# The feed-forward half of a gated cross-attention layer, in four groups of two batches instead of groups of 2, 3 and 3

## The reference, cut to what matters

```python
x = x + tanh(g_xattn) * xattn(ctx, ctx, layernorm(x), Wk, Wv, bv, Wq, bq, Wo, bo)
x = x + tanh(g_ffn) * ffn(layernorm(x), w1, conv_w, conv_b, w2)
# xattn: x is (8, 100, 512), ctx is (8, 722, 512); softmax(q k^T / sqrt(512)) v, one head
def ffn(x, w1, conv_w, conv_b, w2):
    h = bit_linear(x, w1)            # rows quantised to int8 by their largest value, weights to -1, 0, 1
    h = depthwise_conv1d(h)          # 3 taps along the 100 positions of a batch, 2048 channels
    return bit_linear(silu(h), w2)   # the same quantisation, by the largest value of each row of 2048
```

## The kernel before, in words

| section | before | after |
|---|---|---|
| batch 2 | ln2(0), xi, one xqt, rbc(0) | the same (wi(1,3) now stands ahead of the section) |
| batch 3 | second xqt behind res(2); all ff(0), with pt, two kt, pv and three scores between; am1(0) | second xqt and ff(0) from the section's first step, with y, six kt, norm, res(2) and pt between; am1(0) after the first pv; am2(0) after the last; 9 quant(0) among the scores |
| batch 4 | am2(0), 16 quant(0) | 7 quant(0); ln2(1) to rbc(1) at its end |
| batch 5 | ln2(1) to second xqt (three batches) at its end | ff(1) from the first step, with y, kt, norm, res(4), pt, three pv, and f2/out of batches 0 and 1; am1(1), am2(1), 8 quant(1) |
| batch 6 | rbc(1), then behind res(5) all ff(1), with f2/out of batches 0 and 1 and with pt, kt, pv, three scores; am1(1) | 8 quant(1); ln2(2) to first xqt at its end |
| batch 7 | y(6), res(6), am2(1), 16 quant(1) between pt and pv, y(7), res(7) | rbc(2), y(6), res(6), all ff(2) with f2/out of batches 2 and 3, am1(2), pt, two pv, am2(2), 16 quant(2) around the last two pv, y(7), res(7) |
| behind | ln2(2), f2 of batch 2, ff(2) with f2 of batches 3 and 4, am, quant, f2 all of three | ln2(3), f2 of batch 4, ff(3) with f2 of batch 5, am, quant, f2 all of two |

## Time and profile before

### The profile page before, as it was taken

One profiled execution on the slowest core, in us unless ns is written; L12 is line 12 of the kernel. 1 busy time (PEld: TensorE's weight loads), 2 busy tenths in 40 slices (PEclk: granted clock), 3 DMA queues, 4 the chain that ended last, 5 costly groups with the idle time before them and its releaser, 6 DMA issues. The chain is left out here.

```text
span 364.1 us, 4322 instructions
## 1 busy us (share of the span) xinstructions
PE 284.5 (78%) x1496; PEld 202.1 (56%) x1496; DVE 201.2 (55%) x426; ACT 156.3 (43%) x291; POOL 107.0 (29%) x132
## 2 busy tenths in 40 slices
PE   4944999989979989668799996778958575963284
PEld 2414899756537776538578784445826443531142
DVE  0085232330125137669677445679767854798592
ACT  3003137684367552488441324297631102967000
POOL 1007100024210981133226103053321902534090
PEclk9985599999998999957989997898989875887579
DMA  6999129906695259500421600000000000000002
GB/s 191 222 220 330 77 65 294 199 1 154 167 405 132 68 125 229 136 0 3 117 48 21 143 2 0 1 2 23 2 23 0 0 0 24 1 23 3 20 2 68
DMA packets 27952, 32.20 MB, mean 88 GB/s; under 512 B 17866, under 2 KB 17866, under 8 KB 26779
## 3 DMA queue, kind: packets, MB, share of 16 engines
q1 hardware_dynamic: 27930, 31.93, 32.9%
HBM read 26.09 MB, written 1.64 MB: 76 GB/s over the span
## 5 line engine op out<-in xcount | busy, mean ns | idle before, releaser
L861 POOL TENSOR_TENSOR z<-a,ab 128x300 f32<-128x300 f32 (+1 forms) x48 | 33.5, 698 | 77.3 <-DVE a L1076 77.3
L589 PE MATMUL pvb<-pt,ctx 120*128 120x100 f32 (+1 forms) x384 | 45.3, 275 | 1.8 <-ACT pt L743 1.8
L638 PE MATMUL ff<-xqt,w1t 128*128 128x300 bf16 (+1 forms) x192 | 35.4, 333 | 14.1 <-DVE u L1069 12.0
L589 PEld LDWEIGHTS pvb<-pt,ctx 120*128 120x128 f32 (+1 forms) x384 | 44.2, 191 | 3.8 <-issue 3.6
L568 PE MATMUL sc<-kt,qm 128*100 128x361 f32 x128 | 42.4, 480 | 0.0
L804 ACT ACTIVATE a<-u,convb,conv 128x300 f32<-128x300 f32 (+1 forms) x48 | 28.8, 600 | 18.6 <-DVE u L1069 18.6
L872 POOL TENSOR_SCALAR zq<-z_i 128x300 bf16<-128x300 int8 (+1 forms) x48 | 25.6, 558 | 34.9 <-DVE z_i L1114 34.9
L638 PEld LDWEIGHTS ff<-xqt,w1t 128*128 128x128 bf16 x192 | 19.9, 114 | 26.8 <-DVE u L1069 18.8
L549 PE MATMUL tr<-ident,ctx 120*128 120x120 f32 (+1 forms) x192 | 30.0, 281 | 3.9 <-ACT kt L722 3.2
L1076 DVE SCALAR_TENSOR_TENSOR a<-u,conv,a 128x297 f32<-128x297 f32 (+1 forms) x48 | 27.3, 569 | 7.9 <-ACT a L804 7.6
L549 PEld LDWEIGHTS tr<-ident,ctx 120*128 120x128 f32 (+1 forms) x192 | 24.7, 151 | 12.4 <-ACT kt L722 4.2
(11 more groups left out here) (156 smaller groups left out, 474.2 us busy)
## 6 DMA issues: line engine op xcount, KB each, us to landing
ctx<-in_ctx_dram SPq DMA_DIRECT2D x16, 720.0 KB
wraw<-in_L_ffn_w_dram SPq DMA_DIRECT2D x8, 1024.0 KB, 13.4
x_sb<-in_x_dram SPq DMA_DIRECT2D x2, 800.0 KB
out_dram<-x_sb SPq DMA_DIRECT2D x8, 200.0 KB
wq_sb<-in_L_xattn_Wq_dram SPq DMA_DIRECT2D x4, 256.0 KB, 4.3
wk_sb<-in_L_xattn_Wk_dram SPq DMA_DIRECT2D x4, 256.0 KB, 6.4
wv_sb<-in_L_xattn_Wv_dram SPq DMA_DIRECT2D x1, 1024.0 KB, 4.8
wo_sb<-in_L_xattn_Wo_dram SPq DMA_DIRECT2D x1, 1024.0 KB, 7.4
```

Of the source, the lines that this page charges most:

```text
L589: mm = nc.tensor.matmul(pvb[:, k * S:(k + 1) * S], cx[b % NCTX][0:r, i, k * P:(k + 1) * P], pt[0:r, i, :], start=(i == 0), stop=(i == 5))
L638: mm = nc.tensor.matmul(ffb[j % 2][:, 0:w], w1t[:, j * DK + k, :], xqt[:, k, 0:w], start=(k == 0), stop=(k == DK - 1))
L861: nc.gpsimd.tensor_tensor(z[:, j - 1, 0:w].rearrange("p (b s) -> p b s", b=nb), a1[:, n % NBUF, 0:w].rearrange("p (b s) -> p b s", b=nb), ...
```

## The change

The groups become four of two batches. The widest group is then 200 columns instead of 300, and every buffer with that width (`z`, `u`, `a1`, `ab`, `acc_q`, `acc`, `row_wide`, `xqt`, `zq`, `z_i8`, `diag`) shrinks. `z` and the buffers behind it lie over `wraw`, where the w2 weights wait to be turned; `row_wide` now falls into the part that is still being read, so the wait for `w2t_ok` moves from the first `ff` step of group 0 to the first `rbc`. The cuts of `weave` are new.

```diff
-GROUPS = [(0, 2), (2, 5), (5, 8)]
+GROUPS = [(0, 2), (2, 4), (4, 6), (6, 8)]
...
-FILL_CUTS = [17, 22, 33, 50, 71, 88, 100, 116]
+FILL_CUTS = [17, 22, 36, 58, 80, 104, 128, 160]
...
                 elif kind in ("rbc", "am2"):
                     g = step[1]
                     dve.wait_ge(bc_ps, n_bc)
+                    if kind == "rbc" and g == 0:
+
+                        dve.wait_ge(w2t_ok, 16 * CHUNK)
                     nc.vector.tensor_copy(row_wide[:, 0:cols(g)], yb[:, 0:cols(g)]).then_inc(bcast_ok, 1)
...
                     if g == 0 and j == 0:
-
-                        dve.wait_ge(w2t_ok, 16 * CHUNK)
                         nc.vector.memset(ab[:, :, :, S:S + 1], 0.0)
```

## The result

The changed kernel takes 397.59 us (median of four, 397.06 to 402.36) against 366.57 in the same comparison: a ratio of 1.086, with a 95% interval of 1.080 to 1.093. The forecast had the sign, but 380 us and a range to 388. The change costs 31 us, not 14. Some executions of every kernel fall into a slower state (over 1.5% above its fastest); medians are taken over all executions, ratios over the others alone.

A forecast was written before the change was run, and what follows sets the result against it. TensorE was taken to bound plain attention, VectorE and ScalarE the `ff` chains. Stage terms 5.6 - 1.7 - 7.1 + 28.6 - 14.3 + 2.6 = +13.7 on 366.2 gave 380 us; forecast 375 to 385, range 369 to 388.

The forecast's parts named there:

- the mechanism: Groups 2 and 3: two `ff` chains of 200 columns nearly in the open, against one of 300 before.
- largest term: Batch 7 up to its residual: 50.7 us against 22.1 before, +28.6, with all of group 2 in it.
- the chain alone: Group 2's `ff` chain in batch 7's section, 200 columns with no attention beside it: 25.2 us.
- theory A: Follow-up forecast: an uncovered 200-column chain costs its full length plus work behind it; removing one group saves 36 to 40 us.
- rival of a better overlap: Sections of batches 3 and 5 overlap better, some 20 us below forecast, 360: faster or no change, 14%; partial gain, 12%.
- rival of the instruction count: All groups, VectorE's busy time alone: some 6 us more, ending at 372; no separate chance.
- rival of the costlier waits: `f2` in batches 5 and 7 stops VectorE longer, +7; half clock behind group 2, +3: 390 us, 18%.
- the signs named beforehand: Batch 7's `nmax` within 3 us of 272; wrong if before 262, open chains over 28 us, or `row_wide` waits for DMA.
- the term for what had no row: Products behind chains at lower clock, up to 5 us at each of two places, and extra `kt` copies: +2.6.
- `wi`: `wi(1,3)` ahead of batch 2's exponential: holds it back 2.0 us at most, costs nothing, 2 us either way.
- the last chain: Behind batch 7's residual: chain falls from 32.0 to 24.6 us with one `out` less, -7.4.
- the plain sections: Batches 4 and 6, attention without `ff` chains: 16.8 us each, near the plain 16.6.

The follow-up runs named there:

- `four_wi_back`: Changed kernel with the last `wi` put back behind batch 2's exponential: 393.6 us, ratio 1.077 to the kernel before.
- `four_f2_late`: Changed kernel with the last `wi` put back and batch 5's `f2` moved from behind tile 9 to behind tile 15 of the last group: 390.9 us, ratio 1.064.
- `four_both`: Changed kernel with the last `wi` put back and unread TensorE products at the chains' ends: 390.3 us, ratio 1.064.
- `four_busy_end`: Changed kernel with unread TensorE products only at the chains' ends: 393.0 us, ratio 1.075.
- `four_less_one`: Changed kernel with batches 6 and 7 left without their feed-forward half, so three groups of two: 361.4 us, ratio 0.983.
- `three_newcuts`: Kernel before, with its groups of 2, 3 and 3, given only the new cuts: 381.1 us, ratio 1.043.
- `four_all`: Changed kernel with the last `wi` put back, unread products at chains' ends, and batch 5's `f2` behind tile 15 of the last group: 386.2 us, ratio 1.060.
- `three_busy`: Kernel before with three unread products behind each `ff` tile where `pv`'s bank is free, twenty ahead of group 2's `am1`: 370.3 us, ratio 1.016.

## Why the prediction was right and wrong

**Right: the mechanism and its largest term.** Group 2's chain came to stand in the open; batch 7's section was forecast at 50.7 us and took 53.3, and the chain alone at 25.2 and took 25.15. That these came so close is partly luck. In `four_wi_back` and `four_f2_late`, which have the same steps from batch 3's `nmax` to this residual, the section took 55.2 us and the chain 26.8, with VectorE waiting 2.4 us for the tile behind the second `f2`; and within the section the 3.8 us missed behind the chain are partly made up by a start that was 1.1 us shorter. Taking one group away gave 36 us back, as theory A said. The rival of a better overlap fell: batch 3's section got longer, not shorter. The rival of the instruction count (372) fell too.

**The rival of the costlier waits came nearest, for half of its reasons.** It had 390 us: 7 us more at four `f2`, 3 us more by the clock behind group 2. The clock part is there (3.8 us). The four `f2` cost VectorE waits of 3.6 and 0.7 us in batch 5 and one of 0.7 in batch 7, no more than the sum had for them; the stop that did cost time was at a fifth `f2`, in the last chain. Of the signs named beforehand, batch 7's `nmax` came at 282.2 us instead of within 3 of 272, and one chain in the open took over 28 us. ScalarE's tables were loaded three times more (16 for 13), not two; each load took 1.28 us, as in the earlier trace rows.

**Wrong: the term for what had no row, 2.6 us.** It should have held the lower clock behind the chains. I bounded it by 5 us for each of two places and took about a quarter of the two together, "nearer the low end since such products recovered within one batch". Behind group 0's chain alone it was 5.9 us (16.1 instead of 10.2), behind group 2's 3.8 (20.4 instead of 16.65; `row_wide` came 9.1 us after the chain's end, and 5.4 in `four_both`, which had products in the gap). The upper end was the right end. Behind group 0 it is the most uncertain: with `wi` put back and no products it was 1.4 us. The row that should have told it was in the old profile: `y(7)` after 4.22 us of waiting ran at the lower level to its end, and `am2` behind the last chain stood at 0.50.

**Wrong: `wi`, costed at nothing with 2 us either way.** I had it hold back the exponential by its 2.0 us at most and let that cost nothing, but `norm`, `pt` and 48 `pv` products stand behind it. The wait cost 1.9 us on TensorE and then the clock: 2.8 us in the changed kernel's profile and 7.2 in `four_busy_end`.

**Wrong: the last chain, 24.6 us, took 28.9.** I took over from the old chain that its `f2` are hidden. With a single `f2` left, the list puts it behind tile 9, when TensorE runs at the lower level, and its 5.67 us left VectorE 4.64 us without a tile. Moving it gave 24.9.

**Wrong: the plain sections, 16.8 us, took 18.8 in batches 4 and 6.** I put the scales of the next group into the first `u` alone. They also hold up the `nmax`, because VectorE makes the row quantisation and the diagonals ahead of it. TensorE's and VectorE's rows at the end of batch 4's section:

```profile
210.72 5.03 PE L568 MATMUL sc<-kt,qm 128*100 128x361 f32 x16
```

```profile
215.61 1.22 DVE L899 TENSOR_SCALAR diag<-ident,row_deq 100x100 f32<-100x100 f32 x2
216.74 0.90 DVE L983 TENSOR_REDUCE nmax<-sc 100x1 f32<-100x722 f32 x1
```

The scores ended at 215.75 and `nmax` began 1.0 later. The rest is TensorE's wait for `norm` behind the quantisations (0.7 us) and what follows it. Two other runs bear both out. `four_less_one` has no scales at the end of batch 6's section, only the eight quantisations, and it took 17.8 us (264.85 to 282.69). In `three_newcuts` batch 4's section, with seven quantisations and no scales, took 17.8 too, and batch 5's, with neither, 16.6. So the scales cost 0.9 us and the quantisations 1.3.

What stays open: why the same code at the same place ran at different clocks in different builds (batch 2's section 21.6 or 26.0 us with `wi` moved, the stretch behind group 0's chain 16.1 us in the changed kernel and 11.6 with `wi` put back ahead of it, batch 7's section 51.3 or 53.8 with products). Of the 6 us left between `four_all` and the forecast, 4 are the sections of batches 4 and 6, which nothing in it mends; the rest is a balance of smaller differences, the largest of them batch 7's section (3.1).

## What to carry to other kernels

Splitting a phase into more, narrower groups helps the last one and costs a whole chain wherever a group's input comes so late that no other work is left to stand beside it: count the chains in the open, not the instructions. When a change makes TensorE wait and then gives it a run of short products, price that run at the lower clock first; the wait itself can be the smaller part (1.9 us of it, and 4.9 in the products behind). And where an instruction is moved ahead of another, follow the queue behind it to the engine that sets the pace, even when the moved one is only 2 us long.

## What the runs showed that was not expected

A wait of 1.9 us on TensorE, after a stretch in which it had been idle for 0.8 of 5.6 us (124.36 to 130.00 in `four_busy_end`), was followed by 48 `pv` products at the lower level, 10.45 us instead of 5.57. In the changed kernel the same wait was followed by 6.45. Products that nobody reads can pay for themselves at a chain's end (from group 2's last `acc` to the residual 16.8 us instead of 20.7), and cost time inside the chain although TensorE has idle time there (the last chain of `three_busy`, 34.8 instead of 32.0). In the kernel before, removing waits worth a few microseconds raised the clock of batch 7's section from 0.81 to 0.96 and gave 5.7 us there.
